# Expert results loaded on ScalarE's queue, rows of 144 words, and a new table of ranks, in a two-layer MoE, Mamba and attention kernel

## The reference

```python
x = x + 0.5 * _L0_ffn_ref(_layernorm(x))          # dense + 8 low-rank experts, softmax gate
x = x + _L0_attn_ref(_layernorm(x))               # x + Mamba-2: conv over time, scan over time, 4 heads
x = x + 0.5 * _L0_ffn_ref(_layernorm(x))
x = x + 0.5 * _L1_ffn_ref(_layernorm(x))          # top 2 of 8 experts (176 wide) + a shared expert (352 wide)
x = x + _L1_attn_ref(_layernorm(x))               # linear attention, 16 heads: context = sum over ALL tokens of k v
x = x + 0.5 * _L1_ffn_ref(_layernorm(x))          # the same experts a second time

# in _L1_ffn_ref
scores = softmax(x_flat @ gate_w.T); _, topk_ids = top_k(scores, 2)
gu = einsum('nh,eih->nei', x_flat, experts_gate_up); h = silu(g) * u
expert_out = einsum('nei,ehi->neh', h, experts_down)
out = einsum('neh,ne->nh', expert_out, w) + sigmoid(x_flat @ shared_expert_gate_w.T) * shared
```

## Time and profile before

| | |
|---|---|
| median of 3 runs | 842.06 us (841.09 to 842.87) |
| profiled execution | 838.86 us |
| its span | 837.5 us |
| mean granted clock | 0.975 |
| PE / DVE / ACT / POOL busy | 92% / 68% / 67% / 62% of the span |
| traffic | 60.70 MB, 72 GB/s over the span |

### The profile page before, as it was taken

How to read it: one execution, slowest core, us unless ns; L and a number is a source line. 1 busy time by engine, 2 the same in 40 slices (tenths; PEclk the granted TensorE clock), 3 DMA queues, 4 the chain that set the end, 5 groups by cost and what they waited for, 6 DMA issues and landing times.

```text
span 837.5 us, 15645 instructions
## 1 busy us (share of the span) xinstructions
PE 766.9 (92%) x4762; PEld 604.3 (72%) x4762; DVE 573.4 (68%) x1960; ACT 559.3 (67%) x1305; POOL 516.7 (62%) x650
## 2 busy tenths in 40 slices
PE   7999999998898999988999999999999999997992
PEld 6668668785877776677877758867587876695771
DVE  5387579988899868767648884767975668633112
ACT  4888788796779688676677754685446577533551
POOL 4137527737837763898854487747775565774652
PEclk9998999998999999999999999999999999998997
DMA  9930000001100120212123212311422111217215
GB/s 326 406 140 2 1 1 1 2 2 39 52 1 8 36 61 23 62 42 75 43 71 92 56 52 71 119 30 49 127 65 59 44 49 33 68 57 221 83 58 169
DMA packets 43890, 60.70 MB, mean 72 GB/s; under 512 B 7083, under 2 KB 32939, under 8 KB 43595
## 3 DMA queue, kind: packets, MB, share of 16 engines
q1 hardware_dynamic: 33987, 39.36, 14.9%
q0 software_dynamic: 9536, 19.68, 7.0%
q10 hardware_dynamic: 288, 0.67, 0.2%
HBM read 26.61 MB, written 33.07 MB: 71 GB/s over the span
## 4 chain that ended last, share of the span: by engine, by line
PE 29%; POOL 22%; DVE 19%; issue 14%; DMA 8%; ACT 7%; SPq 0%; POOLq 0%; DVEq 0%; ACTq 0%
POOL sorted_x L1805 10%; PE psum L563 6%; PE psum L834 5%; PE psum L854 5%; POOL sent_y L1815 4%; DMA sent_y<-e_y,e_sx 3%; DVE m_cv L1066 2%; DMA e_sx<-sorted_x 2%; POOL m_ch L1743 1%; PE psum L558 1%; PE psum L643 1%; POOL m_ch L1746 1%; PE psum L876 1%; PE psum L735 1%; DMA c_ys<-sent_y 1%
## 5 line engine op out<-in xcount | busy, mean ns | idle before, releaser
L1815 POOL DMA_INDIRECT sent_y<-e_y,e_sx x170 | 166.9, 982 | 101.0 <-ACT e_y L1643 60.6
L1805 POOL DMA_INDIRECT sorted_x<-g_xn,r_slot x128 | 128.9, 1007 | 38.3 <-issue 28.3
L834 PE MATMUL psum<-gu_w,e_sx 128*128 x340 | 114.4, 466 | 0.7 <-issue 0.3
L1338 DVE TENSOR_TENSOR e_h<-e_h,psum 128x352 f32<-128x352 f32 x88 | 43.5, 505 | 95.8 <-ACT e_h L1635 95.7
L854 PE MATMUL psum<-d_w,e_h 88*128 x680 | 90.6, 280 | 2.6 <-DVE m_ch L1090 1.7
L854 PEld LDWEIGHTS psum<-d_w,e_h 88*128 88x128 f32 x680 | 84.2, 194 | 11.8 <-issue 9.5
L1643 ACT ACTIVATE e_y<-psum,e_sx 128x128 f32<-128x128 f32 x170 | 52.5, 363 | 49.0 <-PE psum L854 46.4
L834 PEld LDWEIGHTS psum<-gu_w,e_sx 128*128 128x128 f32 x340 | 60.1, 192 | 28.7 <-issue 7.1
L558 PE MATMUL psum<-ones 128*128 128x128 f32 x468 | 70.6, 293 | 3.7 <-POOL ones L1839 2.7
L1461 ACT ACTIVATE e_h<-psum 88x512 f32<-88x512 f32 x88 | 49.3, 574 | 36.3 <-PE psum L563 36.1
L558 PEld LDWEIGHTS psum<-ones 128*128 128x128 f32 x468 | 64.0, 207 | 7.2 <-issue 3.0
(11 more groups left out here) (265 smaller groups left out, 1933.9 us busy)
## 6 DMA issues: line engine op xcount, KB each, us to landing
e_sx<-sorted_x SPq DMA_DIRECT2D x82, 130.0 KB, 2.2
sorted_x<-c_ys SPq DMA_DIRECT2D x8, 975.0 KB, 19.7
c_ys<-sent_y SPq DMA_DIRECT2D x14, 512.0 KB, 4.8
sent_y<-e_y,e_sx POOLq DMA_INDIRECT x170, 2.3
sorted_x<-c_ys SPq DMA_DIRECT2D x4, 520.0 KB, 15.9
xs<-in_x SPq DMA_DIRECT2D x8, 256.0 KB, 7.2
sorted_x<-g_xn,r_slot POOLq DMA_INDIRECT x128
out<-xs SPq DMA_DIRECT2D x7, 256.0 KB, 3.7
```

What stands on the lines that cost most here:

```text
L834: last = e.matmul(two.banks[j].tile[:, 0:2 * IEXP], e_xT[k % SXS][:, j, :], gu_w[:, bass.ds(which[j] * (2 * IEXP), 2 * IEXP)], start=True, ...
L1805: e.indirect_dma_start(out=sorted_x[CHAIN_OF[g]], out_offset=bass.IndirectOffsetOnAxis(ap=r_slot[n][:, k, t:t + 1], axis=0), in_=rows[:, j ...
L1815: e.indirect_dma_start(out=sent_y[CHAIN_OF[g]], out_offset=bass.IndirectOffsetOnAxis(ap=e_sx[k % SXS][:, j, DM:DM + 1].bitcast(U32), axis= ...
```

## The change

Three things are changed. The loads of expert results (`sent_rows`) are issued by ACT on its own queue, with the same waits, now at L1695; their planned cost is 0.5 us where it was 0.45. Rows of `sorted_x` have 144 words (576 bytes) where they had 130 (520 bytes); the 14 added words are zeros, set once by six small memsets, and never read. And every table of ranks is new, so that the order of nearly all instructions is new on every engine.

```diff
-SENT = DM + 2
-EMPTY_ROWS = 15
+SENT = DM + 16
+EMPTY_ROWS = 14
...
-COMBINED = [-18183.9, -8653.47, -118270.4, ...
+COMBINED = [-51777.11, -51614.84, -10490669852.54, ...
...
# scalar_program
+            def sent_rows(i, nth, t0, m):
+
+                c = CHAIN_OF[GROUP_OF[i]]
+                n, k = i - START[CHAINS[c][0]], PAIR0[CHAINS[c][-1] + 1]
+                emptied = ("c_add", i - 1) if i < LAST + 2 else ("m_Y", 4 * NBLK - 4)
+                yield (COMBINED[i] + 4.0 + t0, 0.5, ("sent0", sent(0, k)), ("sent1", sent(1, k)), ("sent2", sent(2, k)),
+                       ("sent3", sent(3, k)), emptied)
+                on.wait_ge("sent0", sent(0, k))
...
+                on.wait_ge(*emptied)
+                e.dma_start(rows_of(i)[:, t0:t0 + m, :, :].rearrange("p j k c -> p j (k c)"),
...
+                  + [attn_kv(b) for b in range(NBLK)] + [attn_out(b) for b in range(NBLK)]
+                  + [sent_rows(i, nth, *part) for i in range(ROUNDS * NBLK) for nth, part in enumerate(parts(i))])
...
# gpsimd_program
+            for n in range(KEPT):
+                e.memset(g_xn[n][:, :, DM + 2:SENT], 0.0)
...
# sync_program
-            def sent_rows(i, nth, t0, m):
...
-                yield (COMBINED[i] + 4.0 + t0, 0.45, ("sent0", sent(0, k)), ("sent1", sent(1, k)), ("sent2", sent(2, k)),
...
-                  + [sent_rows(i, nth, *part) for i in range(ROUNDS * NBLK) for nth, part in enumerate(parts(i))]
```

More of the change, by code:

```diff
@@ L98 @@
 ATANH = [2.0 / (2 * k + 1) for k in range(8)]
[L102 to L105, removed]
+FIRST = [-3291.36, -2285.93, -1714.76, -1578.73, -1259.39, -1292.94, 199.43, 1472.34]
@@ L106 @@
+AGAIN = [-904.98, -1374.34, -1478.91, 166.4, 1246.26, 1463.44, 1713.33, 1260.38]
+MAMBA = [-1583.74, -1508.79, -1381.08, -1380.28, -1484.63, 317.16, 1457.76, 1205.79]
+CHUNK_AT = [-1470.46, -1491.93, -1153.79, -1266.03, -1526.6, -1433.72, -1345.45, -1344.52, -1231.13, -1222.35, -1262.81, -1504.43, -1174.15, -1522.83, -1293.34, -1008.44, 303.63, 246.4, 209.89, 212.2, 1210.58, -9617.04, -11836.51, 1371.95, -14390.67, -15258.83, -15229.32, 1979.69, 812.85, 1082.54, -44100.17, -435126.87]
 TAP_STEP = -2.4
@@ L112 @@
[L112 to L115, removed]
@@ L116 @@
[L116 to L117 removed]
+FINISH = [-1215.15, -1513.62, -851.57, -1630.1, 1507.1, 1428.53, 1836.06, 1704.06]
+GATED = [-1419.45, -1169.18, 194.11, 1496.86, 2856.13, 2089.48, 19168.8, -50051891811.9, -147425976559.43, -188211257026.11, -125093646984.43, -125093647038.43, 11458829840062.97, -1207859933362.71, 30105520719302.78, 11448513055847.13]
@@ new lines @@
+SORTED = [-1569.77, 1382.41, 2111.39, -371949430.43, -72223937184.72, -136049041402.91, 19960183437451.56, 8891805401970.8]
+SCATTERS = [355.64, 2852.59, 5516.16, 367785729927.69, -33051503782194.5, -28360102949431.49, -71977366238238.94, -57659878065133.42]
+PAIRED = [1854.79, 1221.46, -252768435977.85, -205073047513.0, 3965735163379.2, -33433256352152.99, 4.167326937034079e+17, -3.923731754125136e+17]
+PACE = [-17.93, 6.55, 43795837196.24, 5660474391.35, -2046891211923.83, 4553461239341.37, -1.0718338315806886e+16, 1.0490147516467274e+18]
@@ new lines @@
+SENDS = [5378.5, -2397593.57, 271840572094.56, -162346430449.86, -208331430670.58, -116254119734297.75, -4.359352012807381e+16, 2.272497131662976e+18]
+COMBINED = [-51777.11, -51614.84, -10490669852.54, 221898559711.4, -195595637813.26, -195924420859.53, 1295716500721.01, -121821303135.88, 1.834655175892047e+17, 1.8166201372215552e+17, 3.789985826929465e+17, 4.273450493577874e+17, 2532.17, -5569.63, -5736.61, -7800.9]
+KV = [1290.27, 1302.17, -77585082852.47, -11052792755.33, -164443149930.97, -165449726777.42, -125093647046.79, -125093647464.42]
@@ L119 @@
+SECOND = [-180713034087.35, -193752076360.43, 105896387909.46, -8765854740.02, -33432959765307.15, -24327314399391.22, -4322198696782.84, 1209.55]
 TAPPED_BY = [sum(len(TAPPED[k // BLK_PER_BATCH]) for k in range(b)) for b in range(NBLK + 1)]
@@ L1682, in scalar_program @@
             e.dma_start(w_proj[:, :], d["w_proj"]).then_inc(*S.up("w_proj", 16))
+            def sent_rows(i, nth, t0, m):
[5 more added lines that the diff above has]
+                on.wait_ge("sent0", sent(0, k))
+                on.wait_ge("sent1", sent(1, k))
+                on.wait_ge("sent2", sent(2, k))
+                on.wait_ge("sent3", sent(3, k))
+                on.wait_ge(*emptied)
+                e.dma_start(rows_of(i)[:, t0:t0 + m, :, :].rearrange("p j k c -> p j (k c)"),
+                            sent_y[c][SPARE:, :].rearrange("(n p t k) c -> p n t (k c)", p=P, t=TILES_PER_BLOCK, k=TOPK)[:, n, t0:t0 + m, :]
+                            ).then_inc(*S.up(results(i, nth)[0], 16, LANDS))
+                yield None
             return ([decays()] + [ffn0(i) for i in range(len(FFN0))] + [mamba(b) for b in range(NBLK)]
@@ L1689, in scalar_program @@
                   + [experts(g, t) for g, t in PAIR_OF]
-                  + [attn_kv(b) for b in range(NBLK)] + [attn_out(b) for b in range(NBLK)])
+                  + [attn_kv(b) for b in range(NBLK)] + [attn_out(b) for b in range(NBLK)]
+                  + [sent_rows(i, nth, *part) for i in range(ROUNDS * NBLK) for nth, part in enumerate(parts(i))])
         def gpsimd_program(e, on):
@@ L1925, in experts @@
                 yield None
-            def sent_rows(i, nth, t0, m):
-                c = CHAIN_OF[GROUP_OF[i]]
-                n, k = i - START[CHAINS[c][0]], PAIR0[CHAINS[c][-1] + 1]
-                emptied = ("c_add", i - 1) if i < LAST + 2 else ("m_Y", 4 * NBLK - 4)
-                yield (COMBINED[i] + 4.0 + t0, 0.45, ("sent0", sent(0, k)), ("sent1", sent(1, k)), ("sent2", sent(2, k)),
[L1933 to L1942, removed]
             def store(b):
```

4 lines of the change are left out of this document (removed).

## The result

| | before | after |
|---|---|---|
| median of 4 runs in the same session | 842.46 us (841.09 to 843.35) | 852.32 us (850.46 to 854.84) |
| profiled execution, its span | 838.86, 837.5 us | 853.42, 852.1 us |
| mean granted clock | 0.975 | 0.964 |

The changed kernel is slower: ratio 1.0131, 95% interval [1.0103, 1.0160]. The forecast was 830.0 us, a gain of 1.4%; the range 815 to 848 us did not hold the time either.

The account below looks back on a forecast made before the run. The prediction saw a kernel of waits between engines, with PE close behind; it summed -13.9 - 4.1 + 2.6 + 1.5 + 1.3 + 0.5 = -12.1 us to a median of 830.0 us, range 815 to 848 us.

Parts of the forecast that it names:

- The new order, up to the last ranking matmul: Ahead of the last ranking matmul, 46 fewer fillers at 0.302 us each shorten the span: -13.9 us.
- Its lower bound: Worst case of the new-order term: nothing gained, if the chip waits in the new places as long as in the old.
- The tail: Behind the last ranking matmul, 27 fewer fillers and SP's queue freed of result loads: -4.1 us, bounds 0 and -8.2.
- Issuing on ScalarE: Twelve result loads among ACT's work at 0.433 us each: half of 5.2 us, +2.6 us.
- waiting: ACT's pair work queues behind waiting result loads: +1.5 us for chain 4, nothing for the other chains.
- Rows of 144: Loads of pairs from sorted_x carry 11% more bytes: +0.5 us, at most 1.8 us.
- Table loads: Two more table loads on ACT, 1.283 us each: half of 2.6 us, +1.3 us.
- memsets: Six memsets of about 0.1 us fall where POOL waits for its first input: nothing; without that cover 0.6 us.
- The gaps come back unfilled: Rival: three quarters of the 13.9 us return as waits without fillers, total 0.0, so 842 us; chance 0.18.
- ACT held up: Rival: at chains 0 to 4 ACT waits for last sends, 5 us each: +11.4, so 853 us; chance 0.13.
- The clock: Rival: fewer fillers lower the tail's granted clock to 0.83, PE grows by 10.3 us: 840 us; chance 0.06.

Follow-up runs that it names:

- e1: Kernel before (result loads on SP, rows of 130 words) with the changed kernel's recorded steps: 847.41 against 841.27 us, ratio 1.0081.
- e4: Kernel before, its order and banks kept, without any of its 234 fillers: 849.31 us, ratio 1.0104 to the kernel before.
- e5: As e1, with its 161 fillers raised in proportion to 234: 849.92 against 843.22 us for the kernel before, ratio 1.0082.
- e17: e6 again, in another session: 840.04 against 840.48 us for the kernel before, ratio 0.9983.
- e6: Kernel before with its old order up to the last ranking matmul and the changed kernel's order behind it: 840.23 us, ratio 0.9977.
- e9: The changed kernel again, in the session where the kernel before took 902.08 us: 908.78 us, ratio 1.0105.
- e12: Changed kernel, its steps and rows of 144 words kept, result loads on SP: 902.02 against 902.08 us for the kernel before, ratio 0.9994.
- e13: Changed kernel with the result loads of chains 0 to 3 on SP: 846.69 against 841.99 us for the kernel before, ratio 1.0069.
- e16: The changed kernel again, as yardstick on the same chip: 851.80 against 841.99 us for the kernel before, ratio 1.0132.
- e2: Kernel before, old steps and rows of 130 words kept, only the result loads issued by ACT: 841.08 us, ratio 1.0006.
- e14: Changed kernel with only chain 4's result loads on SP: 851.36 against 841.99 us for the kernel before, ratio 1.0127.
- e3: Kernel before, old steps and loads on SP kept, only rows of 144 words with the six memsets: 841.03 us, ratio 0.9977.
- e10: e1 again (new order, loads on SP, rows of 130 words): 902.90 against 902.08 us for the kernel before, ratio 0.9991.
- e15: Changed kernel, new order and rows of 144 words, all result loads on SP: 849.77 against 841.99 us for the kernel before, ratio 1.0115.

## Why the prediction was wrong

- **The new order, up to the last ranking matmul: -13.9 us. This step failed.** It counted 46 fillers that went as 46 x 0.302 us of span. The last ranking matmul came at 741.1 us and not near 705: +22.4 us from the 718.7 of before, 14.6 of them from the order alone (733.3 in e1). e4 and e5 show the flaw in the step: fillers lie in gaps, and fewer of them shorten next to nothing. The price was too high as well: 0.302 us holds the overlap with real rows; what a filler had to itself was 51.0 / 234 = 0.218 us, and the time that is not PE's work was 121.7 us and not 141. And the table in the section on the change already held the other half. It has 78 more real matmuls between the last context matmul and the last ranking matmul, a stretch of which the prediction itself says that PE is its bound. I took these as filling a wait; there was none. That stretch grew by 17.8 us. I also wrote that the context is reached with less work done, as if PE led there; it was at 660.8 us, 620 forecast, with DVE's softmax at the end of the chain.
- **Its lower bound.** I gave "nothing" as the worst case, and -27.8 us as the best. A new order can lose as well as gain; the worst case should have been the 78 matmuls at full length, at the prediction's own price about 78 x 0.3 = +23 us, with nothing gained ahead of them. The real rows there came to 15.7 us more.
- **The tail: -4.1 us.** The mechanism can't be told from this, the sign was right: 8.0 us shorter in the changed kernel, near my far bound of -8.2. By itself, in e17, it was worth 2.4 us in the trace and 0.2% in time, an amount that its interval and e6's can't tell from nothing.
- **Issuing on ScalarE, +2.6, and waiting, +1.5 us.** Together the size is about right in the new order: 0.5% or 4.2 us between e1's and the changed kernel's ratio (two sessions, with intervals that overlap), 0.5 and 0.7% in the session of e9 to e12, 0.2% in that of e13 to e16. It is none in the old order (e2). The place was wrong: chain 4 costs nothing that can be told (e14). The waits are 6.0 us and not under 4. So that the sum fits is luck: one term was half of a bound, the other came from a place that costs nothing, and chains 0 to 3, put at nothing, are where e13 hints at a cost. The Trainium skill (DMA: Bandwidth & Descriptors, section on issuing engines that are not separate DMA queues) has it that spreading transfers over engines saves only time to issue. The landings agree, 4.8 us median from either engine; what it costs the engine that issues was for these runs to show.
- **Rows of 144, +0.5 us.** Not to be told from nothing (e3; e10 against e12). Pairs land in 2.2 us as before; the test that I had set, under 2.0 us, did not come in.
- **Table loads, +1.3 us, and memsets, nothing.** 60 table loads stand in the new trace, 58 in the old. No run separates them from the order.
- **Rivals.** "The gaps come back unfilled" (0.18) is the one that held, by its own mark: standing still rose by 19.1 us, over the 10 that I had named. Its price was too small: it let three quarters of the term come back, where all of it did, and the moved work besides. "ACT held up" (0.13) named 853 us, nearly the time, but by 25 us of waits on ACT, where there are 6. "The clock" (0.06) is refuted as a cause by e5.

What stays open: why the order alone lost 0.8% (e1, and e5 on another chip) and 1.15% (e15) and nothing in the one where all kernels ran at 902 us, and which single place in the first 650 us keeps PE waiting; nor does a run keep the order and move the 78 matmuls back, so that their price is read from the stretches and not from an experiment of its own. The waits have grown in many small pieces, and the cut orders did not isolate one.

## What to carry to other kernels

Before you credit a filler, a gap or moved work with time, ask which stretch it lies in and whether that engine is the bound there: run the kernel once without its fillers and once with more of them, and look at the granted clock beside the time, and you know what they are worth. Do not take a filler's busy time for a stretch of its own: where rows overlap, it holds some of its neighbours' time. Charge work at full length where it arrives, if the engine is busy there, and credit it with nothing where it left, if something else leads. A bound of a term that reorders a whole program has to reach to the side of loss.

## What the runs showed of the hardware

- **Idle PE costs clock, and clock costs time.** Without fillers the granted clock fell from 0.975 to 0.941, by 3.5%, and the real rows kept PE busy for 737.7 us in place of 715.8, 3.1% longer. In the tail the clock of e4 was 0.85, against 0.90 in e1 with 102 rows of fillers and 0.95 in e5 with 150 (with the same 102 rows it was 0.93 in the changed kernel and 0.88 in e17, so one trace tells a level only roughly):

```profile
727.00:849.80 122.80, 81.96 (x458) 60.36 (x456) 34.97 (x91) 46.63 (x119) 65.54 (x75) 0.85 0.36 109
```
```profile
731.70:844.40 112.70, 91.47 (x600) 72.95 (x598) 35.91 (x90) 46.39 (x115) 62.10 (x69) 0.95 0.38 117
```

  Yet e5's tail is only 0.7 us shorter than e1's 113.4: more clock helps little where PE waits anyway.
- **An issue on ACT is short.** 336 ns median, where SP took 433. Twelve of them are 4.0 us.
- **The same program, 7% apart.** The kernel before took 840 to 843 us in four of the experiments' sessions and 902 us in one. In that session PE's waits include single ones of 12.3 us that no engine or transfer in the trace released, as in the changed kernel (e9), and the views put waits of other engines down to "remote", a releaser that this core's trace doesn't hold (the page's chain calls it another core or an unknown queue). All four traces of that session have such waits, and none of the other sixteen:

```profile
PE psum L563 <- issue: 22.5, 8, 12.3
PE psum L854 <- issue: 8.9, 6, 5.1
```
```profile
DVE xs L1209 <- remote: 30.2, 4, 16.6
```

  What caused it no trace shows; the new order's loss was not to be seen in that session. A small ratio wants a second session before it is believed.
